# Attention's transfers in SP's queue: whole and free running, or halved and each behind an earlier landing

## The reference, cut to what matters

```python
q = Wq @ layernorm(x) + bq;  k = Wk @ ctx + bk;  v = Wv @ ctx + bv      # 128 x 1024 each, 8 heads of 16 channels
k, v padded by 8 and 7 times;  window t = times t .. t+15
attn = softmax over the window of (q_t . k_window) / 4
x = x + tanh(g_xattn) * (Wo @ sum(attn * v_window) + bo)
```

## Time and profile before

| | |
|---|---|
| median of 3 runs | 1617.93 us (1617.93 to 1624.52) |
| the profiled execution, its own time | 1623.17 us |
| its span in the profile | 1621.4 us |
| mean granted TensorE clock | 0.985 of full speed |
| busy, share of the span | PE 95%, VectorE 90%, GpSimd 78%, ACT 65% |
| attention | the first 420 us or so |
| HBM | 113.92 MB read, 16.78 MB written |

### The profile page before, as it was taken

The page is one execution under the profiler, slowest core; times in us unless marked ns, Lnnn a source line. Parts: engine busy times, 40 slices in busy tenths (PEclk is TensorE's granted clock), DMA queues, the critical chain, the costliest instruction groups (busy, mean ns, idle before and its releaser), DMA issues.

```text
span 1621.4 us, 38499 instructions
## 1 busy us (share of the span) xinstructions
PE 1534.6 (95%) x15590; PEld 789.4 (49%) x15590; DVE 1454.5 (90%) x1425; ACT 1057.2 (65%) x1207; POOL 1262.2 (78%) x948
## 2 busy tenths in 40 slices
PE   6888898988799999999999999999999999999996
PEld 4565566665444444444444444444444444444444
DVE  4688788887798999999999999999999999999997
ACT  3677777877566666666666666666666666666652
POOL 3677677778455988888888888888888888888865
PEclk7899999999899999999999999999999999999999
DMA  4676766775353767666667676666666676666569
GB/s 126 171 155 140 172 145 148 173 159 138 118 143 98 152 154 155 152 151 152 147 153 156 156 155 151 149 153 152 152 155 156 144 156 156 153 152 151 116 182 324
DMA packets 192267, 250.16 MB, mean 154 GB/s; under 512 B 14446, under 2 KB 138030, under 8 KB 192074
## 3 DMA queue, kind: packets, MB, share of 16 engines
q1 hardware_dynamic: 167994, 164.26, 36.8%
q0 software_dynamic: 22752, 82.85, 29.1%
q10 hardware_dynamic: 1344, 0.59, 0.2%
HBM read 113.92 MB, written 16.78 MB: 81 GB/s over the span
## 4 chain that ended last, share of the span: by engine, by line
PE 86%; ACT 5%; issue 4%; POOL 2%; DVE 1%; DMA 1%; SPq 1%; ACTq 0%; DVEq 0%; POOLq 0%
PE bank L1193 69%; PE bank L1111 3%; PE bank L1100 2%; ACT pT L684 2%; PE bank L1066 2%; PE bank L1131 2%; PE bank L1073 2%; PE bank L1062 2%; PE bank L1058 1%; ACT vn_hl L662 1%; POOL oacc L628 1%; PE bank L1078 1%; PE bank L1090 1%; ACT pr L679 1%; ACT xn L692 1%
## 5 line engine op out<-in xcount | busy, mean ns | idle before, releaser
L988 DVE SCALAR_TENSOR_TENSOR acc<-bank,scale,acc 128x1024 f32<-128x1024 f32 x784 | 969.5, 1279 | 51.7 <-PE bank L1193 14.9
L1193 PE MATMUL bank<-xT,w_int 128*128 128x512 f16 x3584 | 847.8, 379 | 6.3 <-DVE xT L940 2.0
L628 POOL TENSOR_TENSOR oacc<-oacc,d_part 128x1024 f32<-128x1024 f32 x219 | 536.3, 2454 | 54.5 <-ACT d_part L832 49.0
L1193 PEld LDWEIGHTS bank<-xT,w_int 128*128 128x128 f16 x3584 | 350.3, 98 | 431.4 <-DVE xT L940 3.3
L832 ACT ACTIVATE d_part<-bank,scale 128x1024 f32<-128x1024 f32 x219 | 244.1, 1115 | 200.8 <-PE bank L1193 196.9
L1193 PE MATMUL bank<-h_hi,d_int 128*128 128x512 f16 x896 | 339.6, 379 | 2.1 <-ACT d_part L832 1.8
L1193 PE MATMUL bank<-h_lo,d_int 128*128 128x512 f16 x896 | 339.6, 379 | 0.0
L832 ACT ACTIVATE d_more<-bank,scale 128x1024 f32<-128x1024 f32 x158 | 176.2, 1115 | 154.4 <-PE bank L1193 154.4
L630 POOL DMA_DIRECT2D oacc<-d_more x158 | 149.9, 949 | 114.0 <-ACT d_more L832 107.8
L564 POOL TENSOR_TENSOR raw_z<-raw_w,raw_z 128x512 int32<-128x512 int32 x168 | 225.6, 1343 | 16.5 <-DMA raw_z<-in_L_ffn_gate_z_dram 8.3
L684 ACT ACTIVATE pT<-bank 96x1024 f16<-96x1024 f16 x128 | 130.2, 1017 | 38.3 <-PE bank L1111 37.9
(11 more groups left out here) (85 smaller groups left out, 1438.5 us busy)
## 6 DMA issues: line engine op xcount, KB each, us to landing
oacc<-d_more POOLq DMA_DIRECT2D x158, 512.0 KB, 5.0
raw_w<-in_L_ffn_gate_w_dram SPq DMA_DIRECT2D x56, 256.0 KB, 3.4
raw_z<-in_L_ffn_gate_z_dram SPq DMA_DIRECT2D x56, 256.0 KB, 4.2
raw_w<-in_L_ffn_up_w_dram SPq DMA_DIRECT2D x56, 256.0 KB, 3.4
raw_z<-in_L_ffn_up_z_dram SPq DMA_DIRECT2D x56, 256.0 KB, 4.0
raw_w<-in_L_ffn_down_w_dram SPq DMA_DIRECT2D x56, 256.0 KB, 3.1
raw_z<-in_L_ffn_down_z_dram SPq DMA_DIRECT2D x56, 256.0 KB, 3.7
vt<-vn_hl SPq DMA_DIRECT2D x64, 198.0 KB
```

The costliest lines, as they stand in the source:

```text
L628: nc.gpsimd.tensor_tensor(into, into, d_part[:, (n - 1) % 2, :], ALU.add).then_inc(d_added, 1)
L988: nc.vector.scalar_tensor_tensor(out=into, in0=pair[u % 4][:, :, :].rearrange("p h r -> p (h r)"), scalar=scale[:, par, i, m, k:k + 1], in ...
L1193: last = nc.tensor.matmul(dst[:, h, :], weights, rows_of(h, part), start=(part == 0), stop=(part == 1))
```

## The change

Each load of x and ctx and each row store becomes two issues of 64 partitions, with a semaphore for each half. k's eight moves count on four semaphores in turn, v's twelve on three. With these the queue waits for landings: a move of k, from the fifth on, for the move four before it; a move of v for the move three before it. The first two transfers of each group (`room`) wait for the last ones of the group before it: k's first two for the two halves of the row store, ctx's halves for k's last two moves, v's first two for the halves of ctx, x's halves for the last two moves of v's first copy, the first two moves of v's second copy for the halves of x. `load_x` stands between v's two copies now. All readers wait for all semaphores of a group where they waited for one. `load_x(0)`, `load_ctx(0)`, `load_x(1)` and `load_ctx(1)` ahead of the loop are halved too, without a wait. In the diff `load_ctx` and `keep_row` are left out: they change as `load_x` does.

```diff
-        V_MOVES = 16 * 2 * (VW + 2)
+        V_MOVES = 16 * 2 * (VW + 2) // 3
...
+            PARTS = (slice(0, P // 2), slice(P // 2, P))
-            def load_x(b):
+            def load_x(b, room=()):
                 if b >= 4:
-                    sp.wait_ge(row_kept, 16 * (b - 3))
+                    for half in row_kept:
+                        sp.wait_ge(half, 16 * (b - 3))
                     sp.wait_ge(row_normed, b - 3)
                 if b >= 2:
                     sp.wait_ge(x_normed, b - 1)
-                sp.dma_start(rows[b % 4][:, :], x_in[b]).then_inc(x_loaded[b % 2], 16)
+                for n, wait in enumerate(room or (None, None)):
+                    if wait:
+                        sp.wait_ge(*wait)
+                    sp.dma_start(rows[b % 4][PARTS[n], :], x_in[b][PARTS[n]]).then_inc(x_loaded[b % 2][n], 16)
...
-            def move_k(b, halves=(0, 1)):
+            def move_k(b, halves=(0, 1), room=()):
...
                 for h in range(HG):
                     for hg in halves:
+                        i = 2 * h + hg
+                        if i < len(room):
+                            sp.wait_ge(*room[i])
+                        elif b and i > 3:
+                            sp.wait_ge(k_moved[i % 4], 32 * b + 16)
                         lo = GC * hg + HD * h
-                        sp.dma_start(km[b % 2][lo:lo + HD, :, h, PAD:PAD + T], k_hl[lo:lo + HD, :, :]).then_inc(k_moved, 16)
+                        sp.dma_start(km[b % 2][lo:lo + HD, :, h, PAD:PAD + T], k_hl[lo:lo + HD, :, :]).then_inc(k_moved[i % 4], 16)
-            def place_v(b):
+            def place_v(b, copies=(0, 1), room=()):
...
+                        for dst, src in moves:
+                            if i - copy * (VW + 2) < len(room):
+                                sp.wait_ge(*room[i - copy * (VW + 2)])
+                            elif i > 2:
+                                sp.wait_ge(v_placed[i % 3], V_MOVES * b + 16 * (i // 3))
+                            sp.dma_start(dst, src).then_inc(v_placed[i % 3], 16)
+                            i += 1
...
                 if b >= 2:
-                    keep_row(b - 2)
+                    keep_row(b - 2, x_landed(b + 1) if b + 1 < B else ())
...
                 if b + 1 < B:
-                    move_k(b + 1)
+                    move_k(b + 1, room=kept(b - 2) if b >= 2 else ())
                 if b + 2 < B:
-                    load_ctx(b + 2)
+                    load_ctx(b + 2, [(turn, 32 * (b + 2)) for turn in k_moved[2:]])
                 if b + 1 < B:
-                    place_v(b + 1)
+                    place_v(b + 1, (0,), ctx_landed(b + 2) if b + 2 < B else ())
                 if b + 2 < B:
-                    load_x(b + 2)
+                    load_x(b + 2, [(turn, V_MOVES * (b + 1) + V_MOVES // 2) for turn in v_placed[1:]])
+                if b + 1 < B:
+                    place_v(b + 1, (1,), x_landed(b + 2) if b + 2 < B else ())
```

More of the change, by code:

```diff
@@ L181, in flamingo_layer @@
         pad_hi, pad_lo, pad_placed, ones_placed = sem("pad_hi"), sem("pad_lo"), sem("pad_placed"), sem("ones_placed")
-        x_loaded = [sem("even_x_loaded"), sem("odd_x_loaded")]
-        ctx_loaded, k_moved, v_placed, row_kept = sem("ctx_loaded"), sem("k_moved"), sem("v_placed"), sem("row_kept")
+        x_loaded = [[sem(f"{which}_x_half{n}_loaded") for n in range(2)] for which in ("even", "odd")]
+        ctx_loaded = [sem(f"ctx_half{n}_loaded") for n in range(2)]
+        row_kept = [sem(f"row_half{n}_kept") for n in range(2)]
+        k_moved = [sem(f"k_moved{n}") for n in range(4)]
+        v_placed = [sem(f"v_placed{n}") for n in range(3)]
         eps_added, root_taken = [sem("eps_added"), sem("eps2_added")], [sem("root_taken"), sem("root2_taken")]
@@ L381, in load_ctx @@
                     sp.wait_ge(projected, done("v", b - 1, 1))
-                sp.dma_start(ct[:, :], ctx_in[b]).then_inc(ctx_loaded, 16)
-            def move_k(b, halves=(0, 1)):
+                for n, wait in enumerate(room or (None, None)):
+                    if wait:
+                        sp.wait_ge(*wait)
+                    sp.dma_start(ct[PARTS[n], :], ctx_in[b][PARTS[n]]).then_inc(ctx_loaded[n], 16)
+            def move_k(b, halves=(0, 1), room=()):
                 sp.wait_ge(emptied_proj, low_done("k", b, 1))
@@ L401, in place_v @@
                 to = vt[b % 2]
-                for d in (0, KW):
+                for copy in copies:
+                    d, i = KW * copy, copy * (VW + 2)
                     for jj in range(VW):
@@ L405, in place_v @@
                         a, z = max(lo, 0), min(lo + KW, P)
[L406 removed]
+                        moves = [(to[d + a - lo:d + z - lo, slot:slot + NV], vn_hl[a:z])]
                         if lo < 0:
[L408 removed]
+                            moves.append((to[d:d - lo, slot + 1:slot + NV], vn_hl[P + lo:P, 0:NV - 1]))
                         if lo + KW > P:
[L410 to L411 removed]
+                            moves.append((to[d + P - lo:d + KW, slot:slot + NV - 1], vn_hl[0:lo + KW - P, 1:NV]))
+                        for dst, src in moves:
[5 more added lines that the diff above has]
+                            i += 1
             def place_pads():
@@ L419, in place_pads, with keep_row, x_landed, ctx_landed @@
                         sp.dma_start(vt[par][d + KW - PAD:d + KW, slot_of(NJ - 1)], v_pad[0:PAD]).then_inc(pad_placed, 16)
-            def keep_row(b):
+            def keep_row(b, room=()):
                 sp.wait_ge(emptied_proj, low_done("o", b, 1))
-                sp.dma_start(row_dram[b], rows[b % 4][:, :]).then_inc(row_kept, 16)
+                for n, wait in enumerate(room or (None, None)):
+                    if wait:
+                        sp.wait_ge(*wait)
+                    sp.dma_start(row_dram[b][PARTS[n]], rows[b % 4][PARTS[n], :]).then_inc(row_kept[n], 16)
+            def x_landed(b):
+                return [(half, 16 * (b // 2 + 1)) for half in x_loaded[b % 2]]
+            def ctx_landed(b):
+                return [(half, 16 * (b + 1)) for half in ctx_loaded]
+            def kept(b):
+                return [(half, 16 * (b + 1)) for half in row_kept]
             load_x(0)
@@ L458, in first_weights @@
                         sp.wait_ge(projected, done("v", B - 1, 1))
-                        sp.wait_ge(k_moved, 128 * B)
-                        sp.wait_ge(v_placed, V_MOVES * B)
-                        sp.wait_ge(row_kept, 16 * (B - 3))
+                        for turn in k_moved:
+                            sp.wait_ge(turn, 32 * B)
+                        for turn in v_placed:
+                            sp.wait_ge(turn, V_MOVES * B)
+                        for half in row_kept:
+                            sp.wait_ge(half, 16 * (B - 3))
                         sp.wait_ge(scores_ready, S * (B - 1))
@@ L660, in take_high @@
                     if n == 0 and b:
-                        act.wait_ge(v_placed, V_MOVES * b)
+                        for turn in v_placed:
+                            act.wait_ge(turn, V_MOVES * b)
                     nc.scalar.activation(vn_hl[:, 4 * n:4 * n + 4, :, 0:HD],
@@ L666, in take_high @@
                     if n == 0 and b:
-                        act.wait_ge(k_moved, 128 * b)
+                        for turn in k_moved:
+                            act.wait_ge(turn, 32 * b)
                     nc.scalar.activation(k_hl[:, 0, n * HALF:(n + 1) * HALF], src, ACT.Identity, bias=bias[:, 1:2])\
@@ L733, in _ @@
                 lo = GC + HD * h
-                act.dma_start(km[0][lo:lo + HD, :, h, PAD:PAD + T], k_hl[lo:lo + HD, :, :]).then_inc(k_moved, 16)
+                act.dma_start(km[0][lo:lo + HD, :, h, PAD:PAD + T], k_hl[lo:lo + HD, :, :])\
+                   .then_inc(k_moved[(2 * h + 1) % 4], 16)
             for t in first_tasks[2:4]:
@@ L820, in scale_down @@
                     if n == 1:
-                        act.wait_ge(row_kept, 16 * B)
+                        for half in row_kept:
+                            act.wait_ge(half, 16 * B)
                         act.wait_ge(emptied_proj, len(low_place))
@@ L880, in moments_x @@
             def moments_x(b, halves=(0, 1)):
-                dve.wait_ge(x_loaded[b % 2], 16 * (b // 2 + 1))
+                for half in x_loaded[b % 2]:
+                    dve.wait_ge(half, 16 * (b // 2 + 1))
                 if b:
@@ L1054, in project @@
                     if n == 0:
-                        pe.wait_ge(ctx_loaded, 16 * (b + 1))
+                        for load in ctx_loaded:
+                            pe.wait_ge(load, 16 * (b + 1))
                     for m in range(4):
@@ L1084, in scores @@
                 if s == 0:
-                    pe.wait_ge(k_moved, 128 * (b + 1))
+                    for turn in k_moved:
+                        pe.wait_ge(turn, 32 * (b + 1))
                     pe.wait_ge(emptied_proj, low_done("q", b, 1))
@@ L1118, in mix @@
```

(3 more changed lines are left out.)

3 lines of the change are left out of this document (2 added, 1 removed).

## The result

The changed kernel takes 1743.37 us (median of 4, 1741.51 to 1745.57) against 1621.22 for the kernel before (4 runs): ratio 1.073, 95% interval 1.070 to 1.077. It is slower by 122 us where 61 were forecast. The sign, the place and the mechanism were right; the forecast was half of the measured size, and 1743 lies outside 1640 to 1714.

What follows compares the result with a forecast made beforehand. The matmul engine, 95% busy, set 24.04 us a batch; SP's chain of landings would become the bound at 28.5, delaying attention 60.9 us. So 1617.9 + 61 = 1679 us, range 1640 to 1714.

Steps and rivals of the forecast that it cites:

- The loop: SP's queue in the attention stage: a chain of issues and landings of 28.5 us a batch, against 24.04 the engines need.
- the schedule: SP's moves of one batch timed from k0 = 0: v11 lands at 27.55, the next k0 goes at 28.5 us.
- The loads' term: Landing of a half load of x or ctx: 3.9 us, the middle of 3.1 and 4.7, twice in the batch.
- rival B: Half loads in SP's queue take as long as wholes, 4.7 us: 30.9 us a batch, +93 us, 1711; chance 0.10.
- head and tail: Batch 0's first k in the loop stays at 37.98; after batch 14 the weights come at most 1.4 us later, costed at nothing.
- the forecast's 60.9: Delay of ACT's copy of v in batch 14: v's moves land at 433.2, where the copy stands at 372.30 today.
- The clock: Matmul engine in attention: at half clock, 2 us of added work hidden under a 4.5 us wait, so nothing.
- C: SP's chain fits with every term at its floor: 23.7 us a batch, under 24.04, time stays 1618; chance 0.06.
- D: Matmul engine's code blocks wait behind crowded transfers; pacing returns half its "issue" time, 18 us, giving 1600; chance 0.05.

Runs made afterwards that it cites:

- the last run: Changed kernel with whole transfers, k and v paced four under way, no waits between groups, x's load between v's copies: 1623.71 us, ratio 1.000 to before.

## Why the prediction was right about the place and wrong about the size

**What bounds the kernel.** Right as to the place: ACT's copy of v is where the lateness enters, and behind it TensorE's mix. 13 or 14 waits of some 6 us were expected, 60 us more in all; there were 14 of 10.7 us, 150 us. Over the whole span ACT idled 39 us before these copies in the kernel before and 161 us in the changed one: 122 us more, about the whole loss.

**The loop.** Right as a mechanism: SP's in-order queue became a chain of landings; taking out one link of 1.9 us gave back 24 us, and taking out all links and paces gave back all but 1%. The links, forecast and measured from SP's issues, mean of batches 2 to 13 of the changed kernel, us:

```
link                        forecast   measured
k0 to ctx                     7.1        7.5
ctx to v0                     3.9        3.85
v0 to x                       5.95       7.9
x to v6                       3.9        3.8
v6 to row                     4.85       5.7
row to the next k0            2.8        3.1
sum                          28.5       31.9
```

**The step that failed** is this one: "Paced moves have little in front of them, so nearer the lower end: m = 2.6" (m is the time from the issue of a move to its landing, and the schedule has it three times on v's moves). The loads, where I took the middle, came to 3.85; k6, the move of k in the sum, to 2.5. The moves of v did not come to 2.6: v3 leaves 3.5 us after v0 in the mean (3.1 in the median), x's half 3.8 us after v4, v9 3.0 us after v6 even where only v7 and v8 are beside it. v11 then waits for v8 as well and leaves 1.9 us after v9, where the schedule had 1.5. Of the 3.4 us by which the sum is too short, v's two rows make 2.8. SP's issues of v6, v9 and v11 in one batch:

```profile
257.50 0.78 SPq L437 DMA_DIRECT2D vt<-vn_hl  x1
...
260.50 0.54 SPq L437 DMA_DIRECT2D vt<-vn_hl  x1
...
262.01 0.67 SPq L437 DMA_DIRECT2D vt<-vn_hl  x1
```

The records of the landings show it for v6, 40 partitions of 4.2 KB each: besides one early step the semaphore rises in ten steps, not sixteen, six of them 2.4 us after the issue, the last four 2.8 to 3.0 us after. So 40 pieces are shared by ten engines, four to each. A move of 8 partitions, which rises in eight such steps, is whole after a median of 2.4 us (v7), one of 48, in sixteen steps and so three pieces to each engine, after 3.0 to 3.5. Both rows from which I bounded m (2.1 and 3.7) were of v, but I read the lower one (v0's burst over at 379.0) off a half-microsecond window of share, as if the landing followed at once. The run with an eighth of the data shows that data, not SP's waking, made the difference. That is also the answer to the last sign of being wrong that the prediction names, "a loop over 31 because one slow engine of 16 holds every link": the loop is over 31, but the last step of a landing stands behind the one before it by 0.03 us in the mean for v6, 0.04 for v4, and 0.3 to 0.5 for ctx's first half and v0, where now and then one step comes over a microsecond late (v3 left up to 4.9 us after v0). By these means late steps add about 1 us a batch at most. The loads' term, where rival B put its price, was right: halves land in 3.5 to 4.0 us:

```profile
row<-in_x_dram SPq DMA_DIRECT2D x32, 256.0 KB, 4.0
ct<-in_ctx_dram SPq DMA_DIRECT2D x32, 256.0 KB, 3.5
rows_after_attention<-row SPq DMA_DIRECT2D x32, 256.0 KB, 3.2
```

**The sum**. My schedule spaced v's landings from batch 1 to 14 by 28.3 us, (433.2 - 65.5)/13; ACT's copies stand 31.63 apart: 13 x 3.35 = 43.5 us. Two more terms were missing or put at nothing, head and tail. The head:

```profile
24.41 14.88 SPq L437 DMA_DIRECT2D vt<-vn_hl  x12
...
44.84 5.19 SPq L414 DMA_DIRECT2D km<-k_hl  x8
```

v's moves of batch 0 are paced too. I had left SP's first k in the loop at 37.98; it stands at 44.84, +6.9 (4.8 of them the pace, by the run with batches 0 and 15 free), and from there to ACT's copy batch 0 adds 2.2. And the tail:

```profile
487.23 6.31 SPq L414 DMA_DIRECT2D km<-k_hl  x8
493.64 12.46 SPq L437 DMA_DIRECT2D vt<-vn_hl  x12
508.48 0.44 SPq L491 DMA_DIRECT2D raw_w<-in_L_ffn_gate_w_dram  x1
```

From k's first move of batch 14 to the first weights are 21.3 us, where I had 17.9 and today there are 19.0; from ACT's first copy of v in batch 14 to the first weights 22.6 us instead of 17.5, and from it to the end of the span 5.4 more, where I had put the tail at nothing. With the forecast's 60.9: 60.9 + 6.9 + 2.2 + 43.5 + 5.4 = 118.9, and the spans differ by 119.0. The terms come from the same two traces, so this sum must close; it says where the time lies, and the runs above say why.

**The clock.** Costed at nothing under the wait's cover. The granted clock of the stage fell from 0.99 to 0.86 (60 to 400 us), while TensorE waited more. No run changes the clock alone; but the links add up to the loop without it, and with one link less the time fell by 24 us at the same 0.86, so it was not the bound. The DMA share fell from 0.67 to 0.51, further than to the forecast 0.6.

**Rival B** (a half as long as a whole) gave 1711 and was nearer in number, for a wrong reason: L, the landing of a half load, was 3.85, and whole transfers under the same waits were slower, not faster. Where nothing waits for a landing the rule of the Trainium skill ("DMA: Bandwidth & Descriptors", Rules for kernel authors: two partition halves aren't worth splitting) holds: halves alone cost 1.0%, whole ones 0.45%.

**Rivals C and D.** Not this change. C asked for every term at its floor, m = 1.9 among them, and v's moves took 3.0 to 3.8. For D, less "issue" on TensorE once transfers are paced: it fell to 3.3% of the chain, but behind a wait; with only as much pacing as costs nothing (the last run) the ratio is 1.000. So the 18 us are not there to be had this way. The share of "issue" in these 110 us also differs where nothing is paced: 7.3% with whole transfers and no waits, 13.1% with halves. What the 10.9% of "issue" is stays open.

## What to carry to other kernels

An in-order DMA queue that waits for landings is a loop: add issue, landing and issue around it, and compare with what the engines need a batch; idle time of the queue (here 6.3 us a batch) is spent first, and after it each microsecond counts once per batch. Look at head and tail too, where the same helper runs: here they were 14.5 of the 119 us, and the forecast had them at nothing. Price a landing from the shape of that very move, how many engines its partition count allows and how many pieces each gets, not from a burst in a window of DMA share. If transfers must be paced, keep enough under way that issue hides the landing (four moves of k: some 5 us at most; three of v: 16 us here), and don't tie one group's first transfer to the last landing of another.

## What the runs showed of the hardware that was not expected

- Within SBUF, on SP's queue in the changed kernel (medians of batches 2 to 13): 64 KB from 16 partitions land 2.4 to 2.6 us after the issue, and 3.1 to 3.6 for k1 to k3, whose last step often came late; 29 KB from 8 partitions in 2.3 to 2.8, 165 KB from 40 partitions in 3.0 to 3.1, and in 3.6 to 3.7 behind two moves of 48; 198 KB from 48 in 3.0 to 3.5. With an eighth of the data all of these moves of v land in 1.8 to 2.0.
- A half load of x or ctx (64 partitions, 256 KB) landed in 3.5 to 4.0 us, the whole (512 KB) under the same waits in 3.6 to 3.8: half the bytes save next to nothing.
- A DMA of 40 partitions raised its semaphore in ten steps, 2.4 to 3.0 us after the issue; one earlier step, 1.2 us after it, must have made up the rest, for the waits count on 16 for each move.
